# The second norm's rows turned by DMA instead of by TensorE, in a fused audio-tower block

## The reference

```
h = gelu(x[:, 1:] @ W[:256] + x[:, :1] @ W[256:] + b)     # token stage, exact gelu
y = layernorm(h)
h = h + softmax(cosine similarity of y's rows) @ y + y     # first attention, per batch
z = layernorm(h)                                           # the second norm
logits = z/|z| @ sim/|sim| - sigmoid(gates)                # 8 experts
mask = logits > 0, or the two highest where none is
route = softmax over the experts in the mask
q, k, v = sum over experts e of mask[:, e] * (z @ {q,k,v}_proj[e])   # 256 -> 128
a = causal softmax(q k^T / sqrt(128)) @ v
h = h + sum over e of mask[:, e] * route[:, e] * (a @ o_proj[e])     # 128 -> 256
```

## Time and profile before

| | us |
|---|---|
| median of 3 runs (lowest to highest) | 709.33 (708.91 to 710.06) |
| span of the profiled execution | 708.6 |
| TensorE (PE) busy | 703.0, 99% |
| VectorE (DVE) busy | 572.1, 81% |
| GpSimd (POOL) busy | 402.7, 57% |
| ScalarE (ACT) busy | 373.1, 53% |

### The profile page before, as it was taken

How to read it: one execution, slowest core, us unless ns; L and a number is a source line. 1 busy time by engine, 2 the same in 40 slices (tenths; PEclk the granted TensorE clock), 3 DMA queues, 4 the chain that set the end, 5 groups by cost and what they waited for, 6 DMA issues and landing times.

```text
span 708.6 us, 18356 instructions
## 1 busy us (share of the span) xinstructions
PE 703.0 (99%) x5356; PEld 467.6 (66%) x5356; DVE 572.1 (81%) x1456; ACT 373.1 (53%) x808; POOL 402.7 (57%) x669
## 2 busy tenths in 40 slices
PE   9999999999999999999999999999999999999997
PEld 8888666665757666575756666575766656575655
DVE  5888898887979888787979888787988878786736
ACT  4977373554546364553646355454646356364443
POOL 7642326756466566746566575646556674653434
PEclk9999999999999999999999999999999999999999
DMA  9681230303021030302111030303113020301121
GB/s 242 150 190 48 63 78 6 96 2 86 14 67 33 12 88 0 93 7 73 27 47 52 7 93 0 88 12 67 33 18 81 0 93 7 77 26 53 15 75 30
DMA packets 57975, 39.87 MB, mean 56 GB/s; under 512 B 29928, under 2 KB 53720, under 8 KB 57816
## 3 DMA queue, kind: packets, MB, share of 16 engines
q1 hardware_dynamic: 57552, 39.16, 21.8%
q10 hardware_dynamic: 392, 0.32, 0.2%
HBM read 30.45 MB, written 9.01 MB: 56 GB/s over the span
## 4 chain that ended last, share of the span: by engine, by line
PE 97%; DMA 1%; issue 1%; POOL 0%; ACTq 0%; POOLq 0%; DVE 0%; ACT 0%; DVEq 0%
PE bank L1752 77%; PE bank L1815 7%; PE bank L1669 5%; PE bank L1726 3%; PE bank L1658 2%; PE bank L1886 2%; PE bank L1801 1%; PE bank L1674 1%; DMA region_b<-in_x_dram 1%; PE bank L1837 0%; PE bank L1826 0%; PE bank L1829 0%; POOL region_c L699 0%; POOL region_c L692 0%; PE bank L1706 0%
## 5 line engine op out<-in xcount | busy, mean ns | idle before, releaser
L1752 PE MATMUL bank<-xm,w_qkv 128*128 128x374 f16 x2304 | 415.7, 322 | 0.0
L1752 PEld LDWEIGHTS bank<-xm,w_qkv 128*128 128x128 f16 x2304 | 221.4, 98 | 140.9
L961 ACT ACTIVATE region_c<-bank,out_w 128x256 f32<-128x256 f32 x180 | 85.0, 472 | 170.6 <-PE bank L1752 169.5
L1341 DVE TENSOR_TENSOR xm<-xT,mask_all 128x1496 f16<-128x1496 f16 x128 | 154.6, 1230 | 0.1
L1752 PE MATMUL bank<-w_o,aoT 128*128 128x512 f16 x540 | 143.3, 379 | 0.0
L1245 DVE SCALAR_TENSOR_TENSOR h<-bank,out_w,h 128x256 f32 (+1 forms) x180 | 86.0, 478 | 54.7 <-ACT region_c L961 49.1
L692 POOL TENSOR_TENSOR region_c<-region_c 128x512 f32<-128x512 f32 x46 | 78.5, 1706 | 27.8 <-ACT region_c L961 22.8
L729 POOL TENSOR_TENSOR exp_hl<-exp,exp_hl 128x128 f16<-128x128 f32 (+2 forms) x48 | 34.2, 714 | 83.2 <-ACT exp_hl L903 83.2
L1752 PEld LDWEIGHTS bank<-w_o,aoT 128*128 128x128 f16 x540 | 50.0, 98 | 39.6
L699 POOL TENSOR_TENSOR region_c<-region_c 128x256 f32<-128x256 f32 x46 | 46.9, 1019 | 8.1 <-POOL region_c L692 7.9
L1815 PE MATMUL bank<-xhl,exp_hl 128*128 128x257 f16 (+1 forms) x432 | 50.3, 272 | 0.0
(11 more groups left out here) (205 smaller groups left out, 1059.3 us busy)
## 6 DMA issues: line engine op xcount, KB each, us to landing
mask_all<-d_mask SPq DMA_DIRECT2D x32, 384.0 KB, 4.2
h<-in_x_dram SPq DMA_DIRECT2D x16, 256.0 KB, 4.9
out_dram<-h SPq DMA_DIRECT2D x31, 128.0 KB
rnorm_row<-d_rnorm SPq DMA_DIRECT2D x16, 192.0 KB, 3.9
d_v<-xinT SPq DMA_DIRECT2D x14, 192.0 KB, 4.4
xinT<-d_v SPq DMA_DIRECT2D x56, 48.0 KB, 2.3
h<-in_x_dram SPq DMA_DIRECT2D x15, 112.0 KB, 5.6
out_dram<-h SPq DMA_DIRECT2D x15, 112.0 KB
```

The lines of the kernel that those rows point to most:

```text
L961: a.activation(prod[:, prod_buf(n, t), q, :], pair_bank(n, p)[:, C:2 * C], ACT.Copy, scale=weights_out(n)[:, t, 2 * q + 1:2 * q + 2]).then ...
L1341: v.tensor_tensor(xm[:, e, :, 0:T], xT[1][:, :, :, 0:T].rearrange("p a c t -> p (a c) t"), mask_all[:, e, 0:T].unsqueeze(1).broadcast_to([ ...
L1752: last = t_.matmul(dst, left[lp], right[rp], start=(starts and k == 0), stop=(stops and k == 2), skip_group_check=True)
```

## The change

For batches 2 to 15 the twelve TensorE transposes of the second norm's rows and the two copies out of PSUM go. In their place the SP queue, at the start of its step, waits for each part and issues one crossbar DMA transpose of 128 x 768 fp16 (192 KB), SBUF to SBUF, straight into `xT[1]`. `xs[1]` and `xhl[1]` are laid out with the channel block ahead of the tile, so that a transpose reads 768 adjacent elements. Readers of `xT[1]` wait for both DMAs (s_T2_moved). Batches 0 and 1 are turned by TensorE as before. On TensorE logits moves from behind M(12) to behind pair 2 and M(13), and turn_mask from between M(15) and pair 4 to between M(16) and pair 5; VectorE adds pairs 0 to 2 ahead of route. ScalarE's order is as before but for the copy that goes. All waits that raised one of three counters nobody reads now raise one, s_passed.

```
+        def by_queue(b):
+            return not isinstance(b, int) or b > 1
+        def second_rows_turned(engine, f):
+            if by_queue(f):
+                engine.wait_ge(s_T2_moved, 32 * (f - 1))
+            else:
+                engine.wait_ge(s_T2_hi, f + 1)
+                engine.wait_ge(s_T2_lo, f + 1)
...
+            def second_rows_around(f):
+                for p, done in enumerate((s_hi2, s_lo2)):
+                    sp.wait_ge(done, f + 1).then_inc(s_passed, 1)
+                    if p == 0:
+                        sp.wait_ge(s_xm_ready, E * f).then_inc(s_passed, 1)
+                        sp.wait_ge(s_logits_done, f).then_inc(s_passed, 1)
+                    sp.dma_start_transpose(xT[1][:, p, :, :].rearrange("p c (t q) -> p (c t) q", q=P),
+                                           xhl[1][:, p, :, :, :].rearrange("p c t q -> p (c t q)")).then_inc(s_T2_moved, 16)
...
+                if f is not None and not early(m):
+                    second_rows_around(f)
                 if g is not None:
                     norms_out(g)
                     norms_in(g)
...
-                if f is not None:
-                    turned_rows_2(f)
                 if f is not None and n is not None:
                     scale_pairs(0, 4)
...
                     head_low(qT, qkv_bank[0], s_q_hi, m + 1, s_q_lo, qkv_out)
-                    turned_low_2(f)
-                    pairs(0, 2)
+                    pairs(0, 3)
                     route(f)
-                    pairs(2, 4)
+                    pairs(3, 4)
...
-                    M(10)
-                    pe.wait_ge(s_hi2, f + 1)
-                    pe.wait_ge(s_pT_lo, n + 1)
-                    turn_rows(1, f, 0, turn[0], s_turned2_hi)
-                    M(11)
-                    pe.wait_ge(s_lo2, f + 1)
-                    turn_rows(1, f, 1, turn[1], s_turned2_lo)
+                    M(10, 11)
                     pair(n, 0)
                     pair(n, 1)
                     M(12)
+                    pair(n, 2)
+                    M(13)
                     logits(f)
-                    pair(n, 2)
-                    M(13, 14)
+                    M(14)
                     pair(n, 3)
                     M(15)
+                    pair(n, 4)
+                    M(16)
                     turn_mask(f)
-                    pair(n, 4)
-                    for k in range(7):
-                        M(16 + k)
-                        pair(n, 5 + k)
+                    pair(n, 5)
+                    for k in range(6):
+                        M(17 + k)
+                        pair(n, 6 + k)
```

More of the change, by code:

```diff
@@ L85, in audio_tower_kernel @@
         small = [sb(f"small{n}", [P, 10 - 4 * n, NT]) for n in (0, 1)]
-        xs = [part(region_b, n * NT * C, NT, C) for n in (0, 1)]
-        xhl = [sb(f"xhl{n}", [P, 2, NT, C + 2 * (2 - n)], F16) for n in (1, 2)]
+        xs = [part(region_b, 0, NT, C), part(region_b, NT * C, NC, NT, P)]
+        xhl = [sb("xhl1", [P, 2, NT, C + 2], F16), sb("xhl2", [P, 2, NC, NT, P], F16)]
         sum_column = sb("sum_column", [P, NT])
@@ L314, in audio_tower_kernel @@
         s_stored = sem("stored")
-        s_pool_passed = sem("pool_passed")
-        s_dve_passed = sem("dve_passed")
-        s_sp_passed = sem("sp_passed")
+        s_passed = sem("passed")
         SPLIT = LAST // 16 * 16
@@ L980, in step @@
                     values_out(m)
-                    high(0, g1)
+                    high_1(g1)
                     output_weights_high(0)
@@ L999, in step @@
                         if f is not None:
-                            high(1, f)
+                            high_2(f)
                         head_high(heads_out(n), probs_bank(n), s_pv_done, n + 1, s_ao_hi,
@@ L1069, in _ @@
             split_in(4)
-            high(0, 0)
+            high_1(0)
             gelu(3)
@@ L1089, in _ @@
             split_in(9)
-            high(1, 0)
+            high_2(0)
             gelu(8)
@@ L1093, in _ @@
             turned_rows_2(0)
-            high(0, 1)
+            high_1(1)
             gelu(9)
@@ L1112, in _ @@
             gelu(14)
-            high(1, 1)
+            high_2(1)
             gelu(15)
@@ L1393, in low_2 @@
                 dve.wait_ge(s_hi2, f + 1)
[L1394 removed]
+                if by_queue(f - 1):
+                    dve.wait_ge(s_T2_moved, 32 * (f - 2))
+                elif later(f):
                     dve.wait_ge(s_turned2_lo, f)
[L1396 removed]
+                v.tensor_tensor(xhl[1][:, 1, :, :, :], xs[1][:, :, :, :], xhl[1][:, 0, :, :, :],
                                 ALU.subtract).then_inc(s_lo2, 1)
@@ L1725, in turn_rows @@
                     for t in range(NT):
-                        last = t_.transpose(as16(dst, NC * TP)[:, c * TP + t * P:c * TP + (t + 1) * P],
-                                            xhl[n][:, part, t, c * P:(c + 1) * P], ident16[:, :])
+                        rows = xhl[0][:, part, t, c * P:(c + 1) * P] if n == 0 else xhl[1][:, part, c, t, :]
+                        last = t_.transpose(as16(dst, NC * TP)[:, c * TP + t * P:c * TP + (t + 1) * P], rows, ident16[:, :])
                 last.then_inc(done, 1)
```

172 lines of the change are left out of this document (90 added, 82 removed).

## The result

The changed kernel takes 720.77 us (720.47 to 721.27, 4 runs) against 709.22 before: ratio 1.0162, 95% interval 1.0147 to 1.0176, 11.5 us slower. The forecast was 716.0, range 708 to 765.

The account below looks back on a forecast made before the run. A loop of TensorE and VectorE, 40.37 us a step, was taken as the bound; 1.51 + 13.91 + 1.55 + 23.88 = 40.85 adds 6.7 us over 14 steps, giving 716.0 us, range 708 to 765.

Parts of the forecast that it names:

- the two waits that were named: TensorE waits each step before pair 0 (0.69 us, for the heads' low part) and before pair 6 (0.66 us).
- my own case: Whole kernel: no late transposes, 714 to 718 us, 716.0 as the forecast time; chance 0.48.
- the transposes queue behind each other: SP queue: second transpose lands 5.5 to 8.9 us after the high part's end, time 718 to 765; chance 0.27.
- The bound: A TensorE and VectorE loop sets the 40.37 us step; TensorE's own work is 40.18, or 39.50 without the transposes.
- Pair 0: TensorE starts it 1.51 us, formerly 1.69, after ScalarE ends the high part (hi2), waiting for VectorE's heads' low part.
- Pair 6: TensorE starts it 2.43 us after turn_mask's start (T), a new 0.66 us wait for pair 4's add.
- VectorE's stretch from pair 8 to hi2: VectorE's work from adding pair 8 to the end of ScalarE's high part, taken as unchanged at 23.88 us.
- My sign of being wrong: DMA traffic slowing VectorE's or ScalarE's work from pair 8 to the high part would show the forecast wrong.
- The sum: Loop per step: 1.51 + 13.91 + 1.55 + 23.88 = 40.85 us, 0.48 more than before, +6.7 us over 14 steps.
- The transposes: SP queue's crossbar DMAs: 3.9 us each, second issued 1.1 us after the high part's end, no wait at logits.
- The rivals that had them late: Transposes delay logits: queued behind each other, 718 to 765 us, chance 0.27; tiles one by one, 777 to 1029, 0.10.
- The mask's trip: The mask's DMA broadcasts after turn_mask: cover shrinks to about nothing without cost; 0.2 us late would cost 2.8 in all.

Follow-up runs that it names:

- e2: Kernel before with only the new order of logits, turn_mask and pair adds, rows still turned by TensorE: 720.26 us, ratio 1.0153.
- g2: f2 with GpSimd's first-norm low part moved between the two sums of tile 0, rows turned by TensorE: 707.68 us, ratio 0.9973.
- g3: Kernel before with only GpSimd's first-norm low part moved between the two sums of tile 0: 707.34 us, ratio 0.9972.
- g1: f1 with GpSimd's first-norm low part moved between the two sums of tile 0, rows turned by crossbar: 702.40 us, ratio 0.9910.
- f3: Changed kernel with low_2's wait for the earlier transposes put ahead of its wait for the high part: 720.62 us, ratio 1.0147.
- e3: Changed kernel with pair 4 scaled ahead of turned_mask on ScalarE and added ahead of weight_max on VectorE: 714.82 us, ratio 1.0073.
- f4: Changed kernel with GpSimd's first-norm low part moved between the two sums of tile 0: 719.00 us, ratio 1.0128.
- e1: Changed kernel with the old order of logits, turn_mask and pair adds, DMA transposes kept: 720.64 us, ratio 1.0157.
- f1: Changed kernel with pair 4 early, the heads' parts ahead of the norm's parts, and output_weights ahead of the heads' low part: 710.00 us, ratio 1.0006.
- f2: The three order repairs of f1 on the kernel with TensorE's transposes, turned behind pairs 0 and 1: 715.38 us, ratio 1.0074.

## Why the prediction was right, and what it missed

The direction was right, and so were the loop and the two waits that were named. The size was low: a loss of 11.5 us where 6.7 was forecast. The 720.77 lies outside the 714 to 718 that I gave my own case, and inside the 718 to 765 of the rival *the transposes queue behind each other*, which did not happen. That the range holds the time is partly luck: it had been widened for a rival, and another cause filled it.

**The bound.** Right: a loop of TensorE and VectorE, not TensorE alone. e2 and the changed kernel differ by 12 transposes a step and by 0.5 us in all. g2 and g3 reach the forecast's figure for TensorE's work, 40.18, to 0.02, and g1 reaches 39.50 plus a wait.

**Pair 0.** Right in place and cause, mis-sized: forecast 1.51 behind hi2, measured 1.69, which is by chance what it was before. low_2 starts 0.13 behind hi2 instead of 0.04, since the wait for the earlier transposes, and the register operation for its value, now come between the two (f3: 0.03 of it goes with the register operation; 0.07 stays, with the one step of the sequencer's that is left). And pair 0 starts 0.14 behind the heads' low part, where I took the 0.06 at which another instruction had followed hi2; why it is 0.14 stays open.

**Pair 6.** Right: forecast T + 2.43, measured T + 2.42; 13.91 from pair 0 to pair 8, measured 252.57 + 41.24 - 279.89 = 13.92. e2 shows that it is the order, e3 that it is pair 4's place behind the mask copy.

**VectorE's stretch from pair 8 to hi2.** This is the term that I had carried over unchanged. Forecast 23.88, measured 24.09. Two things make the 0.21. The new order brings pair 8 0.93 closer to T, GpSimd's low part keeps its distance to T (7.33 before, 7.22 now), and the two meet for longer: 0.83 more in mask_tokens, of which 0.13 is left at the end of the stretch, since VectorE then waits less for TensorE and misses a later meeting (a mask_tokens of 1.41 takes 0.93). e2 has the same without a DMA transpose (+0.12), and f4, without the meeting, gives 0.13 back. The other 0.08 is ScalarE, which starts the high part 0.11 behind norm_apply's end instead of 0.03; e1 has it alone, e2 has it not. My sign of being wrong, that DMA traffic slows this stretch, is not what happened: the transposes are issued behind hi2.

**The sum.** 1.69 + 13.92 + 1.54 + 24.09 = 41.24: +0.87 a step instead of +0.48, and 0.39 = 0.18 + 0.21 from the two terms above. Fourteen steps give 12.2, and from the second turn_mask to the last it is 12.2: the distances at either end of the even ones grow by 1.37, 0.51 (to 40.86) and 0.73 (to 40.89). Behind the last turn_mask the changed kernel is 1.5 shorter (59.80 against 61.27), which leaves 10.7; the profiled spans differ by 10.2, as the first turn_mask also came 0.56 sooner in that execution (55.73 against 56.29). The runs gave 11.5; the 0.8 between is within the spread of the runs of the kernel before (708.91 to 710.06) and of the profiled executions' starts, and is not explained further.

**The transposes.** Taken at 3.9 us, measured 2.8. But the first holds the queue for 1.23 us, so the second goes at hi2 + 1.7 where I had 1.1. It lands at hi2 + 4.5 where I had 5.0. No wait, as forecast. The rivals that had them late were wrong for this kernel and half right for e1. Of the two statements of the Trainium skill, that of "Advanced Engine Details and Errata" (as fast as plain DMAs) is borne out as far as this kernel can show it: 2.8 us against 4.0 and 4.4 for the same bytes, but those go to or from DRAM, and no plain move from SBUF to SBUF stands beside it. The 1309 ns a tile of "VectorE: DVE Perf Modes" cannot be multiplied by the tiles: six land together in 2.8 us, 0.47 a tile.

**The mask's trip.** Its cover was forecast to shrink to nothing without a cost. VectorE shows no wait there in the changed kernel.

## What to carry to other kernels

An engine busy 99% of the time may still be one half of a loop: write the loop down with its terms, and time taken from the busy engine counts only where no other engine's result arrives behind it. When an edit moves one instruction against its neighbours, check what else hung on the old distance: the engines' orders that were not edited (pair 4 on ScalarE), and work of another engine that was less in the way by luck (GpSimd's low part). A wait that is added on the loop costs something even when it is long over: here 0.08 on ScalarE and 0.09 on VectorE a step. Here the offload was worth 5 us, but only once three orders around it had been mended (f1 against f2), and it took a fourth to beat the kernel before; until then the same transposes cost nothing on TensorE.

## What was not expected of the hardware

- A crossbar transpose of 128 x 768 fp16 from SBUF to SBUF lands in 2.8 us, in less time than a plain DMA of the same size to or from DRAM in the same kernel (4.0 and 4.4), but holds the issuing queue for 1.23 us against 0.36.
- GpSimd stops a VectorE operation with two SBUF inputs for the rest of its own instruction: 0.93 us became 2.06 and, in e3, 2.31. 98 of the 128 mask_tokens of the changed kernel end as if they had waited so.
- An instruction starts 0.03 us behind what it waited for where nothing stands between (low_2 before), 0.10 where that wait is a step of the sequencer's own (f3), and 0.13 where a register operation works out the value of a second wait there (the changed kernel).
